# Splitting VectorE's opening and closing of a piece of 4-bit codes over a step of the second attention

## The reference, cut to what matters

```
q = (x @ w_q), k = (x @ w_k), v = (x @ w_v), lk = (x @ w_lq @ w_lk), lv = (x @ w_lv)     # 32 heads of 128
x = _layernorm(x + _causal_attn(q, k, v) @ w_o + _causal_attn(q, lk, lv) @ w_lo)

def nf4_quant_dequant(w):                     # w1, w2, w3 of the last block
    flat = w.reshape(-1, 64)
    absmax = jnp.max(jnp.abs(flat), axis=1, keepdims=True)
    normalized = flat / jnp.where(absmax == 0, 1.0, absmax)
    bounds = (NF4_CODE[:-1] + NF4_CODE[1:]) * 0.5
    idx = jnp.searchsorted(bounds, normalized)
    return (NF4_CODE[idx] * absmax).reshape(shape)
```

## Time and profile before

| | |
|---|---|
| median of 3 runs | 2439.47 us (2437.63 to 2440.76) |
| profiled execution | 2439.4 us, its span 2437.5 us |
| granted clock of TensorE, mean | 0.969 of full speed |
| TensorE / VectorE / ScalarE / GpSimd busy | 92% / 74% / 59% / 65% of the span |

### The profile page before, as it was taken

The page is one execution under the profiler, slowest core; times in us unless marked ns, Lnnn a source line. Parts: engine busy times, 40 slices in busy tenths (PEclk is TensorE's granted clock), DMA queues, the critical chain, the costliest instruction groups (busy, mean ns, idle before and its releaser), DMA issues. The chain is left out here.

```text
span 2437.5 us, 43787 instructions
## 1 busy us (share of the span) xinstructions
PE 2246.6 (92%) x14144; PEld 1993.3 (82%) x14144; DVE 1797.1 (74%) x3270; ACT 1433.7 (59%) x3947; POOL 1577.7 (65%) x1336
## 2 busy tenths in 40 slices
PE   7899999988998899998999999999999999987998
PEld 5788988876886788887888888888888888876886
DVE  5788777767533798888887888888888888964322
ACT  2657676652332567676676676776776766663232
POOL 3556657413444778778878878878788788752343
PEclk8999999988999999999999999999999999998999
DMA  3201111000001101101101111111111011004000
GB/s 101 63 27 42 59 32 43 11 18 1 1 1 55 56 25 54 54 13 61 51 25 50 47 33 51 39 42 50 40 40 52 31 50 40 19 5 146 1 18 18
DMA packets 49555, 95.38 MB, mean 39 GB/s; under 512 B 6768, under 2 KB 14224, under 8 KB 48976
## 3 DMA queue, kind: packets, MB, share of 16 engines
q1 hardware_dynamic: 49296, 92.24, 12.2%
HBM read 81.47 MB, written 10.75 MB: 38 GB/s over the span
## 5 line engine op out<-in xcount | busy, mean ns | idle before, releaser
L1280 POOL TENSOR_TENSOR a_nf_acc<-a_nf_acc,a_nf_term 128x512 f32<-128x512 f32 (+1 forms) x416 | 592.4, 1424 | 142.6 <-ACT a_nf_term L1374 72.0
L1334 ACT ACTIVATE a_probs<-bank,a_dip 128x128 f32<-128x128 f32 (+1 forms) x512 | 208.7, 420 | 192.1 <-DVE a_dip L1615 192.1
L1343 ACT ACTIVATE a_probs<-a_probs,a_share 128x128 f32<-128x128 f32 (+1 forms) x512 | 192.4, 464 | 67.7 <-DVE a_share L1621 67.7
L1799 POOL TENSOR_TENSOR f_w_lo<-WGU,f_w_hi 128x512 fp32r<-128x512 f32 x88 | 112.7, 1302 | 175.0 <-ACT f_w_hi L1810 175.0
L1261 POOL TENSOR_TENSOR a_qk_lo<-a_straight,a_qk_hi 128x512 fp32r<-128x512 f32 (+1 forms) x160 | 193.4, 1211 | 41.3 <-ACT a_qk_hi L1320 41.3
L64 PE MATMUL bank<-a_wo_hi,a_ot_hi 128*128 128x512 f32 x512 | 212.3, 415 | 0.0
L1626 DVE TENSOR_TENSOR a_pt_lo<-bank,a_pt_hi 128x384 fp32r<-128x384 f32 x256 | 141.0, 551 | 91.1 <-ACT a_pt_hi L1351 90.4
L1320 ACT ACTIVATE a_qk_hi<-a_straight 128x512 fp32r<-128x512 f32 (+1 forms) x160 | 94.4, 590 | 184.3 <-DVE a_straight L1600 184.3
L66 PE MATMUL bank<-a_wo_hi,a_ot_lo 128*128 128x512 f32 x512 | 201.2, 393 | 0.0
L65 PE MATMUL bank<-a_wo_lo,a_ot_hi 128*128 128x512 f32 x512 | 200.9, 392 | 0.0
L1685 DVE TENSOR_SCALAR a_nf_term<-a_nf_unit 128x512 f32<-128x512 f32 (+1 forms) x288 | 193.5, 716 | 3.4 <-DVE a_nf_unit L1668 0.6
(11 more groups left out here) (242 smaller groups left out, 8468.0 us busy)
## 6 DMA issues: line engine op xcount, KB each, us to landing
a_raw<-in_l_o SPq DMA_DIRECT2D x64, 256.0 KB, 2.8
a_raw<-in_l_vk SPq DMA_DIRECT2D x32, 384.0 KB, 3.1
a_raw<-in_l_ql SPq DMA_DIRECT2D x32, 320.0 KB, 2.9
a_raw<-in_l_ou SPq DMA_DIRECT2D x32, 288.0 KB, 2.8
a_raw<-in_l_nr SPq DMA_DIRECT2D x16, 384.0 KB, 3.1
a_nf_raw<-in_w_nf SPq DMA_DIRECT2D x24, 256.0 KB, 2.6
coded_w<-a_nf_acc SPq DMA_DIRECT2D x24, 256.0 KB, 2.0
f_codes<-coded_w SPq DMA_DIRECT2D x6, 512.0 KB, 3.9
```

The source lines that it names most:

```text
L1280: pool.tensor_tensor(acc, left, nf_term[:, i % CODE_RING, 0:w], ALU.add).then_inc(nf_added, 1)
L1334: act.activation(probs[:, n % 2, col:col + keys], bank[:, at:at + keys], ACT.Exp, bias=dip[:, n % 2, i:i + 1], accum_out=total[:, n % 2, i ...
L1343: ins = act.activation(cell, cell, ACT.Copy, scale=share[:, n % 2, i:i + 1])
L1799: pool.tensor_tensor(lo, src, hi.bitcast(F32), ALU.subtract).then_inc(part_lo[i], 1)
```

## The change

In a step in which a piece starts, VectorE now does only `code_start` ahead of the shares. Its terms of that step come behind the second `probs_low`, and `code_end` of the piece before comes at the end of the step. In the other steps the terms stay where they were. SP's store of the finished piece is sorted 0.9 of a step later.

```diff
 CODE_RING = 5
+CODE_STARTS = CODE_STEP[::15]
...
                     if not (first and q == 0):
-                        work.append((ended, lambda q=q: code_store(q - 1)))
+                        work.append((ended + 0.9, lambda q=q: code_store(q - 1)))
...
-                def codes(n):
-                    for q in range(PER):
-                        ended = CODE_STEP[15 * q - 1] + 1 if q else 0
-                        if ended == n and not (first and q == 0):
-                            code_end(q - 1)
+                def code_terms(n):
                     for i, step in enumerate(CODE_STEP):
                         q, k = divmod(i, 15)
                         if step != n or CODE_ACT[i]:
                             continue
                         _, w = code_cols(q)
-                        if k == 0:
-                            code_start(q)
                         wait(dve, nf_added, code_slot_free(g, first, i))
...
                     peaks(n)
-                    codes(n)
+                    if n in CODE_STARTS:
+                        code_start(CODE_STARTS.index(n))
+                    else:
+                        code_terms(n)
                     shares(n)
...
                     if not (first and n < 1):
                         probs_low(n - 1, 1)
+                    if n in CODE_STARTS:
+                        code_terms(n)
...
                     for name in units[1:]:
                         unit_low(name)
+                    if n in CODE_STARTS and not (first and n == 0):
+                        code_end(CODE_STARTS.index(n) - 1)
```

## The result

The changed kernel took 2457.91 us, median of 4 runs (2456.47 to 2459.61), against 2440.09 us for the kernel before in the same comparison: ratio 1.0075, 95% interval 1.0058 to 1.0093, 18 us slower. The forecast was no change (2438.6 us), and its range ended at 2456. The time lies just above the range, where rival C, the slower one, had it. The span of the profiled execution is 2457.7 us, the mean granted clock 0.965.

A forecast was written before the change was run, and what follows sets the result against it. VectorE's list, trading work with ScalarE, was taken as the bound, not TensorE. The start steps summed to -0.1 us a group, -0.8 us over 8 groups: 2438.6 us, no change that can be told; range 2416 to 2456.

The forecast's parts named there:

- rival C: GpSimd's sums start later, run back to back without pause, and VectorE's rotations wait: likeliest about 2452 us, up to 2464; 25%.
- TensorE's wait is a symptom: Second attention: TensorE's 33.1 us of waits in six groups cost nothing themselves; each step lasts as long as VectorE's list.
- The sign given for it: TensorE's waits for the low half of the transposed probabilities would fall under 10 us in six groups.
- Step 1 of the walk: Step 5's opening: code_start alone ahead of the shares ends by 3.5 us, so L1626 starts at 3.67, 2.3 us earlier.
- steps 2 to 4 of the walk: Rest of step 5: second L1626 at 7.85 us, terms to 9.45, L1600 and code_end held; next peaks near 14.1, +0.2.
- The sum: Steps 0, 5, 8 and 11 together: +0.1 + 0.2 - 0.4 + 0 = -0.1 us a group, -0.8 us in 8 groups.
- the second sign of being wrong: The prediction is wrong if steps 6 to 10 lengthen while the start steps do not.
- Steps 8, 0 and 11: The other steps where a piece starts: -0.4, +0.1 (middle) and 0 (middle) us a group.
- The store at zero: SP's later store of a finished piece costs nothing, its buffer being next written one whole piece later.

## Why the prediction was wrong

- **That TensorE's wait is a symptom and VectorE's list the bound: right.** The kernels in which TensorE got its low half soonest were not the fastest, and in the steps that grew behind a start VectorE has no idle time left (0.06 us in steps 6 and 10). The sign given for it failed: the waits at L1490 were to fall under 10 us and are 34.7 against 33.1. Those in the start steps more than halved (29.4 to 13.1 us), and new ones came in steps 6 and 9.
- **Step 1 of the walk failed: "I take 3.5. That still fits".** It took the end of L1261 at +2.44 from the trace of before and kept it. The change moved it to 3.90, through step 0, four steps earlier. The first low half came at +4.69 instead of +3.67, and the next `peaks` at 15.34 instead of 14.1. With step 5 changed alone the backlog ends at 2.43 and the step takes 14.31, 0.2 us above the forecast: steps 2 to 4 of the walk, with L1600 and `code_end` both held, were right.
- **The sum failed at what it left out.** It had -0.1 us a group for the start steps and nothing for the rest, a term put at nothing without a reason, though rival C gave one against it. The start steps gave -0.13, +1.44, -0.24 and -0.48, together +0.6 us a group (so step 5 lengthened, and the steps from 6 to 10 that are no start by 1.2 us: the first half of the second sign of being wrong, without its second half); the others +0.96 in steps 1 to 4, +0.46 in 6 and 7, +0.77 in 9 and 10 and 0.04 in 12 to 15, +2.2 in all. The 2.8 us are 22.6 in 8 groups; 19.4 were measured, the outer groups losing less.
- **Rival C had the mechanism and the sign, and its price by luck in part**: GpSimd's idle time ahead of a first sum went from 3.48 to 6.76 us ("about 7"), its idle time in steps 6 and 10 from 2.4 us to 0.7 each (7 and 9 kept 1.2 and 1.1), and the long rotation took 1240 ns in the mean of six groups, near the 0.69 + 0.57 that C reckons with. Its price of +2.1 us a group is close to the +2.2 that the steps with no start lost, but it counts the rotation alone. The terms were held 6.8 us a group more as well, and the waits covered three quarters and not half. It lacked the carry-over to the next start: step 5 lost 1.03 us by it in the changed kernel (15.34 against 14.31), and step 0 another 0.41 (10.09 against 9.68). It stood at 25% though its condition could be read from the trace before. GpSimd idles 3.40 us in steps 1 to 4 of group 3 of the kernel before (1.31 of them in a pause, the rest in the gaps of up to 0.18 us between its operations) and 2.10 in those of the changed one, with no pause. What it lost more at step 0 it took along: its backlog ends 1.46 us later in step 5.
- **Steps 8, 0 and 11** came within a quarter to half a microsecond: -0.24 for -0.4, -0.13 for +0.1, -0.48 for 0. **The store at zero** was right.
- A second cause that the prediction did not price is the cover: codes' work ahead of the first low half fills up to 0.9 us in which VectorE would wait for ScalarE. With GpSimd's sums cut, 9.9 us of the change's cost are left; lost cover is part of them, operations still held beside GpSimd's other work are the rest, and no run tells how much of each. How the 18 us of the full kernels divide between the cover and the backlog stays open too, since the holds fill the same wait (VectorE has none there in step 5 of the changed kernel). The runs with one start at a time can't be added either: +9.2, +9.3 and +17.2 make 36, for the greater part because a start with the old order pays more for a backlog (1.47 and 1.80 us) than one with the new order (1.03 and 0.41).

## What to carry to other kernels

When a piece of work moves later on one engine, ask first when the engine that it feeds gets its first input, and whether that engine has pause enough to make the delay up before its output is next needed; the loss may show several steps away, in a step whose code did not change. Split a move into its halves: here the late terms cost 52 us alone (43 on top of a late `code_end`), the late `code_end` gained 24 us, and the change as made hid that gain. A run that cuts an engine's work shows only what it cuts: look in its trace whether what was to go, here the holds, has gone. A list walked with the releasers' old times is only right while nothing upstream moves.

## What was not expected of the hardware

The steps repeat far more closely than the total: step 7, which no kernel touches, has a median of 9.10 to 9.12 us in all but the one with the terms late and code_end in front (10.27), so the price of an order can be read by step.

The same `code_end` takes 0.68 us where GpSimd pauses and 1.80 where it runs sum after sum with 0.18 us between them, and one term 0.42 or 1.47. In the rows shown it is VectorE that is held, while GpSimd's sums keep their 1.28 to 1.30 us; of all 336 sums of 512 columns in the changed kernel some 60% take up to 1.30 us, and the others up to 1.86. Not every operation in SBUF is held: L1661 (a_nf_top, a TENSOR_REDUCE) took 675 to 744 ns in all its 32 executions, while L1664 right behind it, 8 or 9 columns wide, took from 168 to 1461 ns.

TensorE's granted clock changed places: 0.88 in step 5 before, where TensorE idled 1.86 of 13.90 us, and 1.00 (2.4 GHz) there now, with 0.84, a mix of both levels, in step 6, where it is busy 8.24 of 10.39 us. No step's length is put down to it: step 5 became 1.44 us longer at the higher of the two values, and in step 6 VectorE is busy 10.33 of 10.39 us. That is an argument, and no run tests it.
